# Norm products among dense ones, convolutions one by one, squares on ScalarE, and an earlier work area in a delta-rule attention and spline FFN kernel

## What is computed

```python
q = short_conv(xn @ Wq, conv_wq); k = short_conv(xn @ Wk, conv_wk); v = short_conv(xn @ Wv, conv_wv)
q = q / |q| * 64 ** -0.5; k = k / |k|
beta = sigmoid(xn @ Wb); g = -exp(A_log) * softplus(xn @ Wa + dt_bias)
# per token and head
S = S * exp(g); S = S + k (v - k S) beta; o = q S
o = o * rsqrt(mean(o * o) + eps) * norm_weight * silu(xn @ Wg)
x = x + o @ Wo + (silu(xn @ gate_w.T) * (xn @ up_w.T)) @ down_w.T
# gate_w[2048,512], up_w[2048,512], down_w[512,2048]: cubic splines of control points
```

## Time and profile before

| | us |
|---|---|
| median of 3 runs | 846.13 (845.84 to 847.41) |
| profiled execution | 844.82 |
| its span, first to last instruction | 843.1 |
| TensorE busy | 772.1 (92%) |
| VectorE busy | 576.3 (68%) |
| ScalarE busy | 468.3 (56%) |
| GpSimd busy | 381.4 (45%) |
| mean granted TensorE clock | 0.964 |

### The profile page before, as it was taken

The page is one execution under the profiler, slowest core; times in us unless marked ns, Lnnn a source line. Parts: engine busy times, 40 slices in busy tenths (PEclk is TensorE's granted clock), DMA queues, the critical chain, the costliest instruction groups (busy, mean ns, idle before and its releaser), DMA issues.

```text
span 843.1 us, 15476 instructions
## 1 busy us (share of the span) xinstructions
PE 772.1 (92%) x5688; PEld 450.2 (53%) x5688; DVE 576.3 (68%) x1401; ACT 468.3 (56%) x1078; POOL 381.4 (45%) x415
## 2 busy tenths in 40 slices
PE   2989498998989999989999998998789999999998
PEld 1455276746557656647674655765234444444443
DVE  5899968778887878795878888567865444454400
ACT  3667736654876664684765587657743333333200
POOL 4387887577783654785455777113320000000000
PEclk9989799998999998998999999999999999999999
DMA  7320121321021040003023001075872412222111
GB/s 217 126 88 16 50 65 45 119 63 35 2 70 59 30 151 26 1 0 124 11 101 91 10 1 36 6 229 149 184 185 71 138 50 72 78 63 62 39 51 37
DMA packets 59953, 62.21 MB, mean 74 GB/s; under 512 B 30407, under 2 KB 45116, under 8 KB 59878
## 3 DMA queue, kind: packets, MB, share of 16 engines
q1 hardware_dynamic: 53270, 44.45, 18.7%
q0 software_dynamic: 4224, 13.11, 5.3%
q10 hardware_dynamic: 2384, 3.67, 1.2%
HBM read 33.69 MB, written 19.73 MB: 63 GB/s over the span
## 4 chain that ended last, share of the span: by engine, by line
PE 60%; DVE 24%; issue 5%; POOL 4%; ACT 3%; DMA 3%; SPq 0%; DVEq 0%; POOLq 0%; ACTq 0%
PE bank L665 14%; PE pd L2013 7%; PE pd L2012 7%; PE pd L2011 7%; DVE bank L1154 5%; DVE inv L1160 5%; DVE cv L1071 3%; PE bank L751 3%; PE bank L832 2%; PE bank L742 2%; PE bank L884 2%; POOL rn L1654 1%; PE bank L860 1%; PE pg L1997 1%; DVE BA L1247 1%
## 5 line engine op out<-in xcount | busy, mean ns | idle before, releaser
L665 PE MATMUL bank<-x_parts,w 128*128 128x512 f16 x576 | 137.0, 397 | 1.5 <-DVE x_parts L1028 1.5
L2081 DVE TENSOR_TENSOR hh<-sg,pu 128x512 f32<-128x512 f32 x64 | 44.0, 687 | 92.6 <-ACT sg L2050 91.0
L665 PEld LDWEIGHTS bank<-x_parts,w 128*128 128x128 f16 x576 | 57.7, 102 | 72.8 <-issue 14.1
L1963 POOL DMA_DIRECT2D yr<-y_attn x16 | 8.8, 553 | 189.9 <-DMA out<-yr 189.8
L665 PE MATMUL bank<-w,x_parts 128*128 128x384 f16 x384 | 71.4, 340 | 4.4 <-ACT gate L1398 4.2
L2050 ACT ACTIVATE sg<-pg 128x512 f32<-128x512 f32 x64 | 38.0, 594 | 64.6 <-PE pg L1998 64.5
L1071 DVE SCALAR_TENSOR_TENSOR cv<-raw,taps,cv 128x512 f32<-128x512 f32 x72 | 55.1, 832 | 0.0
L665 PEld LDWEIGHTS bank<-w,x_parts 128*128 128x128 f16 x384 | 36.9, 101 | 34.0 <-ACT gate L1398 6.2
L1654 POOL TENSOR_TENSOR rn<-t,mhalf 128x6 f32<-128x6 f32 x16 | 22.8, 1422 | 65.4 <-DVE t L1240 65.4
L1414 ACT ACTIVATE raw<-bank 128x512 f32<-128x512 f32 x48 | 28.3, 589 | 37.1 <-PE bank L665 35.1
L1154 DVE TENSOR_TENSOR bank<-bank,inv 128x60 f32<-128x60 f32 (+32 forms) x184 | 47.1, 285 | 2.2
(11 more groups left out here) (305 smaller groups left out, 2045.4 us busy)
## 6 DMA issues: line engine op xcount, KB each, us to landing
xr<-in_x SPq DMA_DIRECT2D x16, 256.0 KB, 2.6
y_attn<-xr SPq DMA_DIRECT2D x16, 256.0 KB, 2.3
down_rows<-inv SPq DMA_DIRECT2D x8, 512.0 KB, 5.5
yr<-y_attn POOLq DMA_DIRECT2D x16, 256.0 KB, 2.9
out<-yr SPq DMA_DIRECT2D x16, 256.0 KB, 2.4
xb<-in_x SPq DMA_DIRECT2D x3, 1024.0 KB, 5.2
xn_hi<-x_parts POOLq DMA_DIRECT2D x4, 512.0 KB
xn_lo<-x_parts POOLq DMA_DIRECT2D x4, 512.0 KB
```

What stands on the lines that cost most here:

```text
L665: ins = nc.tensor.matmul(out, a, b, start=first and i == 0, stop=last and i == 2)
L2081: v.tensor_tensor(hh[:, i % 2, :], sg[:, i % 2, :], pu[i % 2][:], ALU.mult).then_inc(h_ready, 1)
```

## The change

- The key norm products are issued one by one between the dense products of the two gate products (one to every second dense product), the query norm products between those of block 7.
- The squares are computed by ScalarE (Square): those of blocks 0 to 2 behind the silus of blocks 1 to 3, that of block 3 between two gate evacuations, those of blocks 4 and 5 after the exponentials of chunk 1.
- In supertiles 1 to 3 VectorE convolves blocks 2 and 3 as a pair, then 4, the output part, 5, the residual, and clears the work area; in supertile 0 GpSimd clears it with the constants.
- The last chunk's diagonals are copied by VectorE in supertiles 1 to 3 (four copies), the others by ScalarE one chunk earlier; block 6 is evacuated ahead of them. The query scales are computed at step 6 of the inversion. The wait for the stored down rows stands at the inversion's end.
- The second half's gates are evacuated after the silu.
- Feature pieces 4 and 5 of the first supertile of `feed`, with their moves, are issued in the end of `attend`; in `feed`'s first supertile the later pieces come two groups earlier; the last turns come later (TensorE at group 5 and not 0).
- The rows of the down weights are stored as [block][high, low][128], 512 bytes a piece, by two DMAs a block; `dw` has the same layout, and the down products read it in four runs of 128 columns.

The diff, cut to its core ("..." stands for what is left out):

```diff
@@ -657,10 +657,15 @@
-  def split_product(out, w_hi, w_lo, x_hi_, x_lo_, swap, first=True, last=True):
+  def out_full(u):
+    return bank[uses[u][0]], full[uses[u][0]]
+  def split_product(out, w_hi, w_lo, x_hi_, x_lo_, swap, first=True, last=True, beside=None):
...
+      if beside is not None and not (last and i == 2):
+        next(beside, None)
@@ -684,17 +689,17 @@
-  def gate_products(s, c, h):
+  def gate_products(s, c, h, beside=None):
...
-                hb == 0, hb == HB - 1)
+                hb == 0, hb == HB - 1, beside)
...
-  def block_products(s, n):
+  def block_products(s, n, beside=None):
@@ -703,7 +708,7 @@
-                x_hi[:, hb, :], x_lo[:, hb, :], False, hb == 0, hb == HB - 1)
+                x_hi[:, hb, :], x_lo[:, hb, :], False, hb == 0, hb == HB - 1, beside)
@@ -712,22 +717,26 @@
-        ins = nc.tensor.matmul(ps[:, at:at + 2], square_of(n)[:, CH * c:CH * c + CH], P.pair[:], start=True, stop=True)
-    return ins
+        yield nc.tensor.matmul(ps[:, at:at + 2], square_of(n)[:, CH * c:CH * c + CH], P.pair[:], start=True, stop=True)
+  def key_norms(s):
+    ps, _ = claim(("sums",), s)
+    for ins in norms(ps, 3 * NCHH, s, 0):
+      yield ins
+      yield None
+  def query_norms(s):
+    ps, _ = claim(("qsums",), s)
+    yield from norms(ps, 0, s, 1)
...
-    ps, f = claim(("sums",), s)
+    ps, f = out_full(("sums",))
...
-      nc.tensor.matmul(ps[:, NCHH * i:NCHH * (i + 1)], mask[:], gv, start=True, stop=True)
-    norms(ps, 3 * NCHH, s, 0).then_inc(f, 1)
-  def query_sums(s):
-    ps, f = claim(("qsums",), s)
-    norms(ps, 0, s, 1).then_inc(f, 1)
+      ins = nc.tensor.matmul(ps[:, NCHH * i:NCHH * (i + 1)], mask[:], gv, start=True, stop=True)
+    ins.then_inc(f, 1)
@@ -909,8 +918,11 @@
+    beside = key_norms(s)
...
-      gate_products(s, i // 2, i % 2)
+      gate_products(s, i // 2, i % 2, beside)
+    for _ in beside:
+      pass
@@ -923,9 +935,13 @@
-      block_products(s, NQK + n)
...
-        query_sums(s)
+        beside = query_norms(s)
+        block_products(s, NQK + n, beside)
+        for ins in beside:
+          ins.then_inc(out_full(("qsums",))[1], 1)
+      else:
+        block_products(s, NQK + n)
@@ -981,6 +997,8 @@
+  start.features(pe, s0, 4, bank[0])
+  start.features(pe, s0, 5, bank[1])
@@ -1118,29 +1136,44 @@
-  def invert_blocks(s):
+  def step(ins):
+    ins.then_inc(t32_step, 1)
+    return t32.next()
+  def clear_inversion(s):
...
-    def step(ins):
-      ins.then_inc(t32_step, 1)
-      return t32.next()
-    if not s.first():
-      dve.wait_ge(downs.down_stored, 32 * s.idx())
...
-    dve.wait_ge(t32_step, step(v.memset(tin, 0.0)))
-    cleared = step(v.memset(tin[:, 0:SUB * SUB:SUB + 1], 1.0))
+    if s.first():
+      t32.next()
+      dve.wait_ge(t32_step, t32.next())
+    else:
+      dve.wait_ge(t32_step, step(v.memset(tin, 0.0)))
+      step(v.memset(tin[:, 0:SUB * SUB:SUB + 1], 1.0))
+  def last_diagonals(s):
+    c = NCH - 1
+    for p in range(len(KQ_HEADS)):
+      ready(dve, ("KQ", c, p), s)
+    for q in range(NSUB):
+      rows = slice(SUB * q, SUB * q + SUB)
+      ins = v.tensor_copy(diag[rows, NH * c:NH * c + NH, :], BA[rows, 0, NH * c:NH * c + NH, rows])
+    ins.then_inc(diag_ready, 1)
+  def invert_blocks(s):
+    cleared = s.val(T32_STEPS, 2)
...
-    query_scales(s)
...
+      if j == 6:
+        query_scales(s)
@@ -1160,6 +1193,8 @@
+    if not s.first():
+      dve.wait_ge(downs.down_stored, 32 * s.idx())
@@ -1266,12 +1301,14 @@
-  def local(s, first, before=None):
-    for n in range(first, NQK, 2):
-      convolve(s, (n, n + 1))
-      if n == 2 and before is not None:
-        residual(before, NCH - 2)
-        og_part(before, NCH - 1)
+  def local(s, before=None):
+    if before is not None:
+      convolve(s, (2, 3))
+      convolve(s, (4,))
+      og_part(before, NCH - 1)
+      convolve(s, (5,))
+      residual(before, NCH - 2)
+      clear_inversion(s)
@@ -1284,6 +1321,9 @@
+      clear_inversion(s)
+    else:
+      last_diagonals(s)
@@ -1321,7 +1361,8 @@
-    start.turned_low(dve, 2, bank[6])
+    start.feature_lo(dve, s0, 4, bank[0])
+    start.feature_lo(dve, s0, 5, bank[1])
@@ -1344,7 +1385,7 @@
-  local(s0, NQK)
+  local(s0)
@@ -1357,7 +1398,7 @@
-    local(s, 2, b)
+    local(s, b)
@@ -1456,6 +1497,10 @@
+  def square(s, n):
+    act.wait_ge(silu_done, s.val(NBLK, n + 1))
+    sc.activation(square_of(n), kq[:, n % NPAIR, n // NPAIR, :], ACT.Square).then_inc(sq_ready, 1)
@@ -1504,7 +1549,10 @@
+      if n >= 3:
+        square(s, n - 3)
...
+    square(s, NQK - 3)
@@ -1512,25 +1560,24 @@
-      if c >= 2:
-        take_diagonals(s, c - 2)
+      if c == 1:
+        square(s, NQK - 2)
+        square(s, NQK - 1)
+      if c >= 1:
+        take_diagonals(s, c - 1)
...
-    take_diagonals(s, NCH - 2)
+    raw_out(s, NQK)
...
-      raw_out(s, NQK)
...
-    else:
-      take_diagonals(s, NCH - 1)
-      raw_out(s, NQK)
...
-      if n in (2, 3):
-        gates(s, 1, n - 2)
...
+      if n in (1, 2):
+        gates(s, 1, n - 1)
@@ -1631,6 +1678,8 @@
+  start.feature_hi(act, s0, 4, bank[0])
+  start.feature_hi(act, s0, 5, bank[1])
@@ -1672,11 +1721,6 @@
-  def square(s, n):
-    pool.wait_ge(silu_done, s.val(NBLK, n + 1))
-    src = kq[:, n % NPAIR, n // NPAIR, :]
-    g_.tensor_tensor(out=square_of(n), in0=src, in1=src, op=ALU.mult).then_inc(sq_ready, 1)
@@ -1701,15 +1745,9 @@
-      if n == NQK - 1 and s.first():
-        square(s, n - 3)
-      if n >= 2 and not (n == NQK - 2 and s.first()):
-        square(s, n - 2)
...
-    square(s, NQK - 2)
-    square(s, NQK - 1)
@@ -1754,6 +1792,9 @@
+  g_.memset(tin, 0.0).then_inc(t32_step, 1)
+  pool.wait_ge(t32_step, 1)
+  g_.memset(tin[:, 0:SUB * SUB:SUB + 1], 1.0).then_inc(t32_step, 1)
@@ -1859,6 +1900,7 @@
+  start.late_turn = bank[6]
@@ -1884,6 +1926,8 @@
+  start.move(sp, s0, 4)
+  start.move(sp, s0, 5)
@@ -1907,7 +1951,7 @@
-    dw = sb("dw", [128, IB, 2, D], F16)
+    dw = sb("dw", [128, IB, NST, 2, 128], F16)
@@ -1922,6 +1966,9 @@
+    def ahead(s):
+  return 2 if s.first() else 0
@@ -1934,7 +1981,7 @@
-  moves(0, range(HB, NP))
+  moves(0, range(HB + 2, NP))
@@ -1973,7 +2020,7 @@
-    gather(dw[:, g].rearrange("p a n -> p (a n)"), g, scr.down, down_in[g % 2])
+    gather(dw[:, g].rearrange("p b a n -> p (b a n)"), g, scr.down, down_in[g % 2])
@@ -2006,11 +2053,11 @@
-    ps, tok, inner = pd[t % 2], slice(CH * t, CH * t + CH), its[s.idx() % 2]
+    ps, tok, inner = pd[t % 2][:].rearrange("p (b n) -> p b n", b=NST), slice(CH * t, CH * t + CH), its[s.idx() % 2]
...
-      nc.tensor.matmul(ps[:], inner[:, 0, i, tok], dw[:, i, 0, :], start=i == 0, stop=False)
-      nc.tensor.matmul(ps[:], inner[:, 0, i, tok], dw[:, i, 1, :], start=False, stop=False)
-      ins = nc.tensor.matmul(ps[:], inner[:, 1, i, tok], dw[:, i, 0, :], start=False, stop=i == IB - 1)
+      nc.tensor.matmul(ps, inner[:, 0, i, tok], dw[:, i, :, 0, :], start=i == 0, stop=False)
+      nc.tensor.matmul(ps, inner[:, 0, i, tok], dw[:, i, :, 1, :], start=False, stop=False)
+      ins = nc.tensor.matmul(ps, inner[:, 1, i, tok], dw[:, i, :, 0, :], start=False, stop=i == IB - 1)
@@ -2021,14 +2068,15 @@
-      if i < 8 - HB:
-        start.features(pe, s, HB + i, pf[i % 2])
-      if s.first() and i == 0:
+      n = i + ahead(s)
+      if HB <= n + HB < NP:
+        start.features(pe, s, HB + n, pf[n % 2])
+      if s.first() and i == 5:
...
-      if following is not None and 6 <= i < 6 + HB:
-        start.features(pe, following, i - 6, pf[i % 2])
+      if following is not None and 6 <= n < 6 + HB:
+        start.features(pe, following, n - 6, pf[n % 2])
@@ -2055,14 +2103,15 @@
-      if 1 <= i < 1 + HB:
-        start.feature_hi(act, s, HB + i - 1, pf[(i - 1) % 2])
-      if following is not None and 7 <= i < 7 + HB:
-        start.feature_hi(act, following, i - 7, pf[(i - 1) % 2])
+      n = i - 1 + ahead(s)
+      if i >= 1 and n < HB:
+        start.feature_hi(act, s, HB + n, pf[n % 2])
+      if following is not None and 6 <= n < 6 + HB:
+        start.feature_hi(act, following, n - 6, pf[n % 2])
...
-      if s.first() and i == 4:
+      if s.first() and i == 6:
@@ -2100,11 +2149,14 @@
-      if 1 <= i < 1 + HB:
-        start.feature_lo(dve, s, HB + i - 1, pf[(i - 1) % 2])
-      if following is not None and 7 <= i < 7 + HB:
-        start.feature_lo(dve, following, i - 7, pf[(i - 1) % 2])
-      if s.first() and i == 5:
+      n = i - 1 + ahead(s)
+      if i >= 1 and n < HB:
+        start.feature_lo(dve, s, HB + n, pf[n % 2])
+      if s.first() and i == 3:
+        start.turned_low(dve, TURNS - 2, start.late_turn)
+      if following is not None and 6 <= n < 6 + HB:
+        start.feature_lo(dve, following, n - 6, pf[n % 2])
+      if s.first() and i == 7:
@@ -2268,6 +2320,7 @@
+    self.dn_rows = inv[:, 1:3, :].rearrange("p i c -> p (i c)").bitcast(F16).rearrange("p (b w) -> p b w", b=IB)
@@ -2325,9 +2378,9 @@
-    rows = self.scr.down.rearrange("(b p) (a n) -> p b a n", p=128, a=2)
```

(5 more changed lines are left out.)

## The result

The changed kernel takes 836.15 us (835.49 to 837.38) against 846.5 us for the kernel before, measured beside it: a ratio of 0.9864, with a 95% interval of 0.9842 to 0.9886, so 10.3 us faster. The forecast was 831.8. The profiled execution is 835.69, its span 833.8 against 843.1. So 9.3 us went where the sum had 14.3.

What follows compares the result with a forecast made beforehand. The chain ending last is 60% TensorE and 24% VectorE, so a stage gives only what its last engine gives. 17.8 + 2.3 - 5.8 = 14.3 us off 844.82 gives 830.5 profiled, 831.8 median; range 825.5 to 838.5.

Steps and rivals of the forecast that it cites:

- Convolutions and squares: Blocks 4 and 5 convolved singly, squares on ScalarE: scores start about 2.1 us earlier in supertile 2, 1.6 in supertile 1.
- Norm products: On TensorE among dense products, each norm product costs 0.13 us, so 12 cost 1.6 instead of 2.9.
- The clock at the scores: TensorE's first score steps: full clock gains 2.1 us in supertile 2, 0.8 in supertile 3; half clock stays in supertile 1.
- C: Rival: scores stay at half clock in supertiles 2 and 3, diagonals take 1.8 us, not 1.2; 835.9; chance 0.17 with F.
- Scores to inversion: From VectorE's last scores to the first inversion step: 3.4 us instead of 5.86; gain 2.6 in each of supertiles 1 to 3.
- The V path: Path from V block evacuation on ScalarE to placing the inverses: gain 5.2 to 7.4 us, taken as 6.2, capping supertile 2's 6.8.
- Supertile 0: Paired convolutions without GpSimd's squares beside them gain 1.0 us of 2.4, the memset done by GpSimd 0.9: 1.9 us.
- Feed: Feature pieces moved into the attention's end, turns later: second feed supertile starts 2.3 us sooner (range 1 to 3.2).
- Given back: TensorE's wait before the solve rises to about 3.6 us; half clock at 75% each in supertiles 1 and 3 loses 5.8.
- D: Rival: two table loads around ScalarE's squares of blocks 4 and 5, about 1 us late in four supertiles; 835.8; chance 0.05.
- The shared port: Cited rule: VectorE instructions with two SBUF inputs share a port with SBUF-reading GpSimd ones; slow adds 1954 against 743 ns.
- F: Rival: norm products wait for late ScalarE squares, dense ones queued behind wait too; counted inside C, 0.17 together.

Runs made afterwards that it cites:

- The run with memsets: Changed kernel with GpSimd's mask products of chunks 0 and 1 in supertiles 1 to 3 replaced by memsets of the same tiles: 825.95 us, ratio 0.976.
- the pair: Changed kernel with VectorE convolving blocks 4 and 5 as a pair behind residual and output part in supertiles 1 to 3: 833.6 us, ratio 0.9831.
- the early masks: Changed kernel plus unused products ahead of the solves, mask products of chunks 0 and 1 behind block 3's halo in supertiles 1 to 3: 821.86 us, ratio 0.9683.
- the pair with the solves' clock held: Changed kernel plus unused products ahead of the solves, blocks 4 and 5 convolved as a pair in supertiles 1 to 3: 822.39 us, ratio 0.9684.
- The bursts run: Changed kernel with norm products in two bursts again, the keys' behind the first differences, the queries' behind block 7: 841.57 us, ratio 0.9945.
- the run with squares on GpSimd: Changed kernel with squares on GpSimd again at their old places, norm products still among the dense ones: 844.81 us, ratio 0.9955.
- further products: Changed kernel with 46, 20, 15 and 15 unused 128x512 products on TensorE ahead of the solves of supertiles 0 to 3: 826.38 us, ratio 0.9757.
- the mix with further products: Changed kernel plus unused products ahead of the solves, blocks 4 and 5 paired in supertile 1, single with masks earlier in 2 and 3: 819.66 us, ratio 0.966.
- the rows alone: Kernel before with only the down weights stored as 512-byte pieces and read in four runs of 128 columns: 846.2 us, ratio 0.9989.

## Why the prediction came out as it did

The direction and the range (825.5 to 838.5) held; the gain was 10.3 us in medians and 9.3 in the spans, where 14.3 was forecast. By its steps:

*Convolutions and squares: the step that failed.* The prediction left "0.9 that I leave for GpSimd's mask product beside them" for block 4 and had its convolution end 3.6 us behind the halo. It took 5.2: two masks of 1.47 us lie beside it, not one, and they add 1.13 us to the multiply and 1.23 to the adds. Forecast 2.1 us in supertiles 2 and 3, measured 0.8; forecast 1.6 in supertile 1, measured 0.0, since with the squares gone the mask of chunk 2 moved up beside block 5's adds (3.42 us), while that of chunk 1 held block 4's; the gather beside the latter cost them nothing that shows. Those are 4.2 us. I had counted the slow adds as freed with the squares, though in the kernel before it was a mask that lay beside blocks 4 and 5's, and I asked what goes, not what stays or moves up in GpSimd's order into the place. The run with memsets shows the mechanism, the pair shows that splitting was a loss by itself, and the early masks and the pair with the solves' clock held put it at 4 to 4.5 us by the medians.

*Norm products.* 0.13 us each, as taken.

*The clock at the scores.* Right in place and size: 1.00 in supertiles 2 and 3, 2.3 and 1.1 us (2.1 and 0.8), and half clock still in supertile 1 (0.50), whose scores took 0.8 us longer, which had no term. The bursts run shows that the norms' place is needed for it, and the run with squares on GpSimd that it isn't enough. The reason given for C, that the clock falls with any weak stretch ahead, says too much: it was 1.00 behind waits of 2.48 and 2.76 us, in two solves of the kernel before.

*Scores to inversion.* 3.2 us in supertiles 2 and 3 (3.4). In supertile 1 4.1: its four copies took 1.93 us in place of 1.04, in the middle of my bounds (0.7 to 3.0).

*The V path* ended 5.8 us sooner in supertile 2 and held nothing up; the 6.2 I capped by was never tested, since the gain ahead of it was 5.7.

*Supertile 0.* 0.6 for 1.9: its six adds went from 6.83 to 6.48 us and not to 5.8, for the same reason as above: the masks of chunks 1 and 2 both lie beside them.

*Feed.* 2.2 in the span (2.3), 1.7 by the run that undoes it.

*Given back.* The wait ahead of the solve is 3.47 us in supertiles 2 and 3, as forecast (3.6), and 4.63 in supertile 1. The solves of 1 and 3 lost 2.1 and 1.4 us, 3.5 in all for 5.8, and the recurrence of supertile 0 lost 1.4, which had no term. I can't say why it did in this run: a stretch of half clock lies at 122 to 125 us there (0.55), in other runs at 139, and in some at neither.

*Sum and range.* That the time fell 4.4 us from the forecast and not further is in part luck: the 2.3 us that the solves kept made good a part of the 4.2. The range's upper end, 838.5, is C or D with 2.5 us; with both C and D, as it is worded, the sum would be 839.9 before any unknown term.

*The table sets.* Rival D is out. The rule of the Trainium skill ("ScalarE: Activation LUTs", "Table sets: the hidden batching unit") asks for batches by set; here the trace shows the 24 squares among exponentials and among silus without a load of their own, with four loads before the exponentials and nine before the silus in both kernels. *The shared port.* The other rule ("SBUF — State Buffer", "Who interferes with whom") was cited as agreeing and not used for a price. It was the one that mattered: the adds have two inputs in SBUF and are held by a reading GpSimd instruction and not by a memset, as that section of the Trainium skill has it; the traces agree (3.56 us beside a mask product, 2.33 beside a memset). By it, the mask product beside the adds should have been priced at about its own time. That the multiply, which has one input, is held as well, by a mask product (1.62 us) and by a memset (0.87), is a second effect, which the traces show and the rule of two inputs doesn't cover.

Of the rivals, C came nearest in time (835.9, with D at 835.8), but hardly for its reasons: the scores of supertiles 2 and 3 went to full clock, and the diagonals were quick in these two; only supertile 1's took about the 1.8 us that C had. The longest wait ahead of a norm product was 0.35 us, in supertile 0, so F didn't happen.

## What to carry to other kernels

When work leaves an engine, lay out the order of what stays: what was queued behind it moves up, and may land on the very instructions that were to be freed. Price every GpSimd instruction that reads SBUF at up to its full time where it lies beside VectorE's multiplies or adds (here 1.1 to 1.2 us for one of 1.47), and put it beside a wait. A gain that lengthens TensorE's idle time can be paid back in part in its clock: fill that time with products whose results nobody reads, where a bank is free.

## What the runs showed of the hardware

- The solve, 378 records of small products, ran in 16.5 us at a granted clock of 1.00 with 0.2 to 0.5 us of idle time ahead, and in 18.0 to 19.5 us at 0.84 to 0.91 with 3.5 to 4.6 us ahead. Behind waits of 1.2 to 2.8 us it fell either way, five times 1.00 and four times 0.80 to 0.90. 15 further products (3.4 us) were worth up to 2.9 us.
- Behind the bursts of norm products, which the profile counts as busy, the scores ran at 0.55 and 0.72. With the same products among dense ones they ran at 1.00 behind a wait of 0.80 us, and at 0.68 behind one of 2.23.
- The same program falls on either side: the kernel with pairs ran in 835.86 us at a mean clock of 0.965 and in 831.06 at 0.973, while the mix with further products stayed within 819.23 to 819.94.
- A memset of 768 columns on GpSimd takes 0.73 us and leaves VectorE's two-input adds at pace (2.33 us for three), but holds up a one-input multiply (0.87 for 0.49). A two-input product of the same size takes 1.47 and holds up both (3.56 and 1.62). It is held up itself where an add is under way: 2.00 us in place of 1.47.
- A moving operand of four runs of 128 f16 columns has no price that shows: the down products follow each other at 0.21 to 0.22 us, and the rows alone gave a ratio of 0.9989 (0.9969 to 1.001).
